# Relu and square of each hidden block made one up product later on ScalarE

## The reference

```python
h = relu(hidden @ up_w) ** 2            # 896 x 2048, up_w is 1024 x 2048
shared_out = h @ down_w                 # 896 x 1024
routed_out = (x_latent @ expert_w * sum of the top 2 logits) @ fc2_w
x = x + layernorm(shared_out + routed_out, gamma, beta)
```

## Time and profile before

| | us |
|---|---|
| median of 3 runs | 1740.98 (1740.56 to 1741.75) |
| the profiled execution: time of its run | 1740.49 |
| its span, first to last instruction | 1738.5 |
| TensorE busy | 1707.8 (98% of the span) |
| VectorE / GpSimd / ScalarE busy | 1027.9 / 960.5 / 739.2 |
| up stage, first product to last | from 1430.1 to about 1588.6 |
| down stage on TensorE | from 1593.0 to about 1731 |

### The profile page before, as it was taken

The page is one execution under the profiler, slowest core; times in us unless marked ns, Lnnn a source line. Parts: engine busy times, 40 slices in busy tenths (PEclk is TensorE's granted clock), DMA queues, the critical chain, the costliest instruction groups (busy, mean ns, idle before and its releaser), DMA issues.

```text
span 1738.5 us, 24780 instructions
## 1 busy us (share of the span) xinstructions
PE 1707.8 (98%) x8539; PEld 1504.3 (87%) x8539; DVE 1027.9 (59%) x1520; ACT 739.2 (43%) x1417; POOL 960.5 (55%) x775
## 2 busy tenths in 40 slices
PE   9999999999999999999999999999999998888998
PEld 8988998899999988888988898889888987777887
DVE  3611112743433458775777577767657368757988
ACT  3311212233434357734773477247512224446342
POOL 2366463445555548875767576736534235566565
PEclk9999999999999999999999999999999999999999
DMA  8788876566677668844763576325223117633444
GB/s 270 229 279 270 275 283 217 167 192 221 208 228 240 216 217 299 285 126 148 248 206 120 168 236 207 119 90 174 64 85 110 49 39 228 194 104 103 133 145 157
DMA packets 214295, 319.37 MB, mean 184 GB/s; under 512 B 20304, under 2 KB 174416, under 8 KB 213328
## 3 DMA queue, kind: packets, MB, share of 16 engines
q1 hardware_dynamic: 214224, 318.49, 56.3%
HBM read 211.78 MB, written 106.66 MB: 183 GB/s over the span
## 4 chain that ended last, share of the span: by engine, by line
PE 92%; DVE 3%; POOL 2%; issue 1%; ACT 1%; DMA 1%; SPq 0%; DVEq 0%; POOLq 0%; ACTq 0%
PE bank L2272 28%; PE bank L2273 28%; PE bank L2274 28%; PE bank L2496 5%; DVE act_region_unrounded L2094 1%; PE bank L2358 1%; POOL slab_raw L1174 1%; POOL tile_region_rounded L1183 1%; DVE small_region_unrounded L2094 0%; DVE y_region L2076 0%; PE bank L2637 0%; PE bank L2344 0%; PE bank L2315 0%; DMA act_region_unrounded<-in_slabs 0%; POOL act_region L1183 0%
## 5 line engine op out<-in xcount | busy, mean ns | idle before, releaser
L1090 POOL TENSOR_TENSOR tile_region<-tile_region,small 128x487 f32<-128x487 f32 x224 | 221.1, 1025 | 72.1 <-DVE small L1775 72.0
L2272 PE MATMUL bank<-mid_region 125*128 125x448 f32 (+5 forms) x612 | 249.3, 407 | 0.1
L2273 PE MATMUL bank<-mid_region 125*128 125x448 f32 (+5 forms) x612 | 230.5, 377 | 0.0
L2274 PE MATMUL bank<-mid_region 128*128 128x488 f32 (+3 forms) x576 | 216.2, 375 | 0.0
L1361 ACT ACTIVATE tile_region<-bank,small 128x487 f32<-128x487 f32 x224 | 153.8, 687 | 30.3 <-DVE small L1779 30.3
L1056 POOL TENSOR_TENSOR slab_raw<-slab_raw 128x256 f32<-128x256 f32 x128 | 98.5, 773 | 120.6 <-DMA slab_raw<-in_slabs 112.9
L1393 ACT ACTIVATE mid_region<-bank 125x512 fp32r<-125x512 f32 x224 | 136.7, 613 | 54.5 <-PE bank L2496 54.4
L1779 DVE TENSOR_REDUCE small<-bank 128x1 f32<-128x487 f32 x224 | 145.8, 652 | 20.8 <-PE bank L2274 20.8
L1830 DVE TENSOR_TENSOR mid_region<-bank,mid_region 125x512 fp32r<-125x512 f32 x224 | 151.6, 682 | 9.3 <-ACT mid_region L1393 9.3
L2272 PE MATMUL bank<-mid_region,act_region 128*125 128x512 f32 (+2 forms) x366 | 143.4, 392 | 2.9 <-DVE y_region L2076 2.9
L2496 PEld LDWEIGHTS bank<-ident,tile_region 128*125 128x125 f32 x896 | 131.3, 187 | 15.9 <-POOL tile_region L1090 2.1
(11 more groups left out here) (311 smaller groups left out, 4288.5 us busy)
## 6 DMA issues: line engine op xcount, KB each, us to landing
slab_raw<-in_slabs SPq DMA_DIRECT2D x112, 256.0 KB, 3.8
q_scratch<-y_region SPq DMA_DIRECT2D x16, 1792.0 KB, 8.1
mid_region<-q_scratch SPq DMA_DIRECT2D x32, 896.0 KB, 6.8
slab_raw<-in_slabs SPq DMA_DIRECT2D x48, 512.0 KB, 3.4
weight_sums_scratch<-slab_raw SPq DMA_DIRECT2D x32, 512.0 KB, 4.3
small_region_unrounded<-in_slabs SPq DMA_DIRECT2D x52, 256.0 KB, 4.8
v_scratch<-slab_split SPq DMA_DIRECT2D x8, 1536.0 KB, 7.8
slab_raw<-weight_sums_scratch SPq DMA_DIRECT2D x48, 256.0 KB, 4.6
```

The source lines that it names most:

```text
L1090: pool.tensor_tensor(PR[i][:, 0:KEYS], PR[i][:, 0:KEYS], rrow[:, i:i + 1].broadcast_to([P, KEYS]), ALU.mult).then_inc(s_pn, 1)
L2272: pe.matmul(out_ap, w[0], a[0], start=first, stop=False)
L2273: pe.matmul(out_ap, w[1], a[0], start=False, stop=False)
L2274: return pe.matmul(out_ap, w[0], a[1], start=False, stop=last)
```

## The change

In step 4 of a pair ScalarE no longer makes a hidden block. Block 0 moves to step 5, blocks 1 and 2 to step 6, and block 3 to step 0 of the next pair, in each place behind the high part that the step makes. For the last pair, block 3 stands behind the loop. Nothing else is moved, and no instruction is added or taken away.

```diff
-                    if n == 4:
+                    if n == 0 and p > 0:
+                        hidden_block(p - 1, 3)
+                    if n == 5:
                         hidden_block(p, 0)
-                    if n == 5:
-                        hidden_block(p, 1)
-                        hidden_block(p, 2)
                     if last and n == 5:
                         down_hi(0)
                     if n == 6:
-                        hidden_block(p, 3)
+                        hidden_block(p, 1)
+                        hidden_block(p, 2)
+            hidden_block(F_PAIRS - 1, 3)
             chunk_hi(0, 3)
             ride_hi(0, 0)
             down_hi(1)
```

## The result

| | us |
|---|---|
| before, median of 4 runs | 1741.0 (1740.56 to 1741.75) |
| changed kernel, median of 4 runs | 1730.17 (1728.92 to 1731.08) |
| ratio | 0.9937, 95% interval 0.992 to 0.9954 |
| the profiled execution: time of its run, span | 1730.59, 1728.6 |

A forecast was written before the change was run, and what follows sets the result against it. TensorE, busy for nearly all of the 1738.5 us span, was taken as the bound, so only its waits could be won. The terms sum to 9.9: 1740.98 - 9.9 = 1731.1 us, range 1726.8 to 1737.0.

The forecast's parts named there:

- pair 1: Up stage, bound by VectorE: 1.9 us won; 2.3 if combination 2 escapes GpSimd's port lock, 1.1 less if caught.
- pair 2: Up stage, bound by VectorE: 1.1 us won; 1.6 if combination 2 escapes GpSimd's port lock, 0.5 if caught.
- pair 3: Up stage, same chain as pair 4: 1.1 us won, with the lower clock's cost of 1.7 left in.
- pair 4: Up stage: an earlier weight chain starts product 6 at 1529.7, not 1532.31; 2.6 us won.
- pairs 5 to 7: End of the up stage: 1.4 us won in pair 5, 0.3 in pair 6, nothing in pair 7.
- seam: Passage to the down stage: its start moves from 1593.04 to 1591.5, 1.5 us won; bounds 2.9 and 0.7.
- wait A: TensorE's wait ahead of product 6 on VectorE's combination 3, 1.94 us idle in pair 4.
- B: TensorE's wait ahead of product 3 on GpSimd's low part 3, 1.29 us idle in pairs 4 and 5.
- B, absorbed: Rival: VectorE's chunks hold pairs 1 to 3 as before; only 4.6 us won, 1736.4; chance 0.18.
- C, the port: Rival: GpSimd catches combination 2 in pairs 1 and 2 and both chunk_lo; 7.8 us won, 1733.2; chance 0.14.
- D, slower: Rival: block 3 delays high part 4 by 1.15 us in each of 7 pairs; 1747.5; chance 0.05.
- E: Rival: ScalarE's order is not on the path, so nothing changes, 1740.98; chance 0.05.

The follow-up runs named there:

- e1: The changed kernel plus one ScalarE wait for combination 4 in step 4 of each pair, block 0's work staying in step 5: 1734.7 us, ratio 0.9966.
- e5: The kernel before, with VectorE's down weight sums cut from 256 columns to 8 per instruction (result wrong): 1722.37 us.
- e2: The kernel before with block 0 alone moved to step 5, ahead of blocks 1 and 2: 1736.82 us, ratio 0.9979.
- e7: The changed kernel with block 3 back in step 6, behind block 2: 1732.59 us, ratio 0.9954.
- e10: The kernel of e8 once more, run beside the unaltered changed kernel on one chip: 1726.16 us, ratio 0.991.
- e3: The changed kernel with the last pair's hidden blocks in their old order: 1732.06 us, ratio 0.9951.
- e6: The changed kernel, with VectorE's down weight sums cut from 256 columns to 8 per instruction (result wrong): 1719.65 us.
- e9: The changed kernel once more, unaltered, beside e10 on the same chip: 1730.57 us, ratio 0.9941.
- e4: The changed kernel with VectorE's chunk_lo(0, 1) moved behind combination 7: 1728.81 us, ratio 0.9935.
- e8: The changed kernel with chunk_lo(0, 1) behind combination 7 and, in the last pair, down_hi(0) ahead of block 0: 1726.69 us, ratio 0.9926.

## Why the prediction was right

Step by step, what was forecast to be won and what was:

| step | forecast | measured |
|---|---|---|
| pair 1 | 1.9 (1.2 to 2.3) | 22.11 - 20.68 = 1.4 |
| pair 2 | 1.1 (0.5 to 1.6) | 22.40 - 20.70 = 1.7 |
| pair 3 | 1.1, or 2.8 without the spell | 21.08 - 18.51 = 2.6 |
| pair 4 | 2.6 | 20.94 - 18.22 = 2.7 |
| pairs 5 to 7 | 1.7 | 11.59 - 8.4 - 1.0 = 2.2 |
| seam | 1.5 | 4.45 - 3.43 = 1.0 |
| in all | 9.9 | 11.6 |

- **The cause.** The weight chain of the next pair behind hidden blocks that wait for combination 4. The rows of pair 4 after show it; e1 (the bare wait brings wait A back, 5.3 of 11.59 lost) and e5 (without the chunks the order costs almost nothing) bear it out. The prediction named the wait of block 0 ahead of high part 1 as what is moved out of the way. That is not all of it: block 0 moved by itself gives under half (e2), since high part 2 then stands behind blocks 0, 1 and 2. The price of each move alone was not measured.
- **Pair 4.** Low part 3, high part 4, low part 4, the chunk, the catch of combination 2 and product 6 came in the order and nearly at the distances of the walk; 18.22 against 18.3.
- **Pairs 1 and 2** were rightly taken as VectorE's: they still take 20.7, with 19.1 of VectorE in them, and e5 takes them to 17.4. What counts there is, as the prediction had it, which of GpSimd's instructions fall on VectorE's: sum 1 left the chunks. But "losing B there only lengthens A" is not what happened: A stayed, and part of B's time came back ahead of product 5. And **pair 1 is mis-sized**: combination 2 was not caught there (0.62), for which the walk had 2.3, and 1.4 was won. The prediction also counted on low part 4 no longer behind low part 3; in pair 1 it took 0.69 before already. In pair 2 before, VectorE also waited 0.59 for a transfer of down weights; how much of that pair's 1.7 is due to this is not shown.
- **Pair 3: mis-sized.** "With that cost left in" was the wrong side: no spell came behind pair 2, so the term is 2.6 and not 1.1. Nor had the spell cost its full 1.7 before: pair 3 had it in place of wait B, and took 21.08 where pair 4 without a spell took 20.94.
- **The seam: mis-sized.** The catch of `chunk_lo(0, 1)` was forecast, by 0.8 behind GpSimd, and came so. What was missed is that the port works both ways: GpSimd's instruction took 3.04 and not 2.45, since `chunk_lo(0, 0)` had started first. That is most of what the term lacks. That the spell behind the seam would stay was the value taken.
- **The sum** hit the time more closely than its terms deserve: 1.7 more was won in the stretch, and the up stage began 1.6 later in that execution. That the two cancel is luck. By the medians, 10.8 were won.
- **The range.** Its lower end is said to be with all catches missed, but takes the seam at 1.5 + 1.7; by the prediction's own bound for that case it is 2.9 + 1.7, and the end 1725.4.
- **The rivals.** B, absorbed, is out: pairs 1 to 3 took 5.7 less. C, the port, is out in pairs 1 and 2. D, slower: high part 3, which waits for sum 2, came 2.4 earlier behind product 6 (6.21 against 8.61), and e7 shows the place of block 3 to be worth nothing either way. E is out.

## What to carry to other kernels

On an in-order engine look at what stands behind a waiting instruction, and at who waits for that: an operation that waits and feeds nobody soon should stand behind the one that feeds a chain. Price such a delay at the end of the chain that it feeds, not at the first wait that shows up: here the visible wait on GpSimd was 0.27 in e1, and the pair still lost 1.8. And where two engines' instructions exclude each other, a transfer or product at a seam should hang on as few of them as possible: e10 took 4.4 us by moving two lines.

## What the runs showed of the hardware

A wait of some 2 us ahead of product 6 is followed by TensorE's lower clock level in one execution and not in another. In pair 1 the wait was 1.98 in the changed kernel and 1.98 in e3; the first kept 2.4 GHz, the second had 9 matmuls shown 0.56 to 0.57 us long in place of 0.37, which start 0.37 apart in place of 0.20. That is 1.6 us, but the pair became only 1.1 longer (21.79 against 20.70), since the waits behind the spell became shorter (0.78 and 1.92 against 1.13 and 2.04). At the seam the waits of 3.05 (e1) to 4.45 were followed by a spell in every profile that had one (before, changed, e1, e2, e3, e5, e6, e7, e9), 2.18 in e4 and 0.71 in e8 and e10 were not.

The exclusion of GpSimd and VectorE works in both directions, also for full-size instructions: VectorE's 0.95 became 3.10 under GpSimd's, and GpSimd's 2.43 became 3.04 when VectorE's had started 0.12 earlier. The Trainium skill (SBUF — State Buffer, section "SBUF: two separate sides") says that whichever starts first holds the shared port pair for its whole instruction. The trace agrees, with these 3.10 and 3.04.
